# A message-passing layer on one core: attribute transfers issued at the landings of scatter pairs

## What is computed

```
row, col = src, dst
tp = fctp_messages(x[col], edge_attr, W1, W2, W3, W4)
messages = tp @ Wm + bm
agg = segment_sum(messages, row, num_segments=N_NODES)
upd = concatenate([x, agg], axis=-1) @ Wu + bu
out = layernorm(x + (x + upd))
```

## Time and profile before

| | us |
|---|---|
| median of 3 runs | 1928.22 (1927.52 to 1932.37) |
| profiled execution | 1923.78 |
| its span, first to last instruction | 1922.0 |
| PE busy | 1660.2 (86%) |
| DVE busy | 1549.8 (81%) |
| POOL busy | 1079.2 (56%) |
| ACT busy | 894.5 (47%) |

### The profile page before, as it was taken

One profiled execution on the slowest core, in us unless ns is written; L12 is line 12 of the kernel. 1 busy time (PEld: TensorE's weight loads), 2 busy tenths in 40 slices (PEclk: granted clock), 3 DMA queues, 4 the chain that ended last, 5 costly groups with the idle time before them and its releaser, 6 DMA issues.

```text
span 1922.0 us, 35044 instructions
## 1 busy us (share of the span) xinstructions
PE 1660.2 (86%) x11964; PEld 894.9 (47%) x11964; DVE 1549.8 (81%) x1727; ACT 894.5 (47%) x1721; POOL 1079.2 (56%) x837
## 2 busy tenths in 40 slices
PE   5439999999999999999999999999999999378883
PEld 2214444444444444444444444444444444266662
DVE  6347888888888888888888888888888886089994
ACT  1204444444444444444444444444444444168885
POOL 3106666766666666666666666666666665301110
PEclk9779999999999999999999999999999999789997
DMA  9996777777777777777777777777777774799994
GB/s 378 405 377 181 232 232 226 231 230 230 230 228 231 231 230 231 229 230 231 235 234 236 235 237 234 237 225 239 239 234 235 231 230 99 237 361 420 418 412 178
DMA packets 174616, 490.06 MB, mean 255 GB/s; under 512 B 48664, under 2 KB 99096, under 8 KB 149484
## 3 DMA queue, kind: packets, MB, share of 16 engines
q1 hardware_dynamic: 91980, 379.42, 51.6%
q0 software_dynamic: 82304, 109.12, 27.3%
q10 hardware_dynamic: 288, 0.95, 0.2%
HBM read 393.10 MB, written 96.31 MB: 255 GB/s over the span
## 4 chain that ended last, share of the span: by engine, by line
DMA 39%; issue 20%; POOL 20%; PE 11%; DVE 5%; ACT 2%; SPq 1%; POOLq 1%; ACTq 0%; DVEq 0%
DMA agg<-summed,row_idx 25%; POOL agg L324 14%; POOL xg L307 6%; DMA prod<-agg 5%; DMA xg<-in_x_rows,dst_sb 4%; DMA agg<-start_rows 4%; PE ps L648 3%; PE ps L641 2%; DVE stats L585 2%; DVE prod L566 2%; DMA e_sb<-in_e_rep 1%; ACT spread L365 1%; PE ps L694 1%; PE ps L629 1%; PE ps L695 1%
## 5 line engine op out<-in xcount | busy, mean ns | idle before, releaser
L324 POOL DMA_INDIRECT agg<-summed,row_idx x392 | 642.2, 1638 | 448.9 <-DMA agg<-summed,row_idx 294.0
L505 DVE TENSOR_TENSOR prod<-ps,e_sb 128x2048 f32<-128x2048 f32 x294 | 663.7, 2285 | 136.8 <-PE ps L648 132.2
L648 PE MATMUL ps<-prod,packed_sb 128*32 128x512 f32 x3136 | 752.7, 603 | 0.8 <-ACT S_sb L377 0.8
L307 POOL DMA_INDIRECT xg<-in_x_rows,dst_sb x392 | 410.5, 1047 | 179.4 <-issue 117.8
L641 PE MATMUL ps<-prod,packed_sb 128*32 128x512 f32 x2352 | 394.3, 600 | 0.0
L365 ACT ACTIVATE spread<-xg 128x1536 f32<-128x1536 f32 x98 | 145.5, 1485 | 424.1 <-DMA xg<-in_x_rows,dst_sb 413.5
L513 DVE TENSOR_TENSOR prod<-ps,e_sb 128x3072 f32<-128x3072 f32 x98 | 328.1, 3348 | 0.0
L493 DVE TENSOR_TENSOR prod<-ps,e_sb 128x2048 f32<-128x2048 f32 x98 | 223.9, 2285 | 108.6 <-ACT A_sb L371 69.4
L648 PEld LDWEIGHTS ps<-prod,packed_sb 128*32 128x32 f32 x3136 | 148.6, 109 | 156.7 <-issue 156.7
L629 PEld LDWEIGHTS ps<-packed_sb,spread 128*128 128x128 f32 x1176 | 127.3, 143 | 172.2 <-issue 123.6
L377 ACT ACTIVATE S_sb<-ps 128x512 f32<-128x512 f32 x98 | 58.7, 599 | 277.8 <-PE ps L648 277.8
(11 more groups left out here) (62 smaller groups left out, 1748.6 us busy)
## 6 DMA issues: line engine op xcount, KB each, us to landing
e_sb<-in_e_rep SPq DMA_DIRECT2D x98, 1536.0 KB, 7.2
e_sb<-in_e_rep SPq DMA_DIRECT2D x98, 1024.0 KB, 5.6
agg<-start_rows SPq DMA_DIRECT2D x49, 640.0 KB, 17.1
prod<-agg SPq DMA_DIRECT2D x48, 640.0 KB, 10.7
out<-prod POOLq DMA_DIRECT2D x48, 640.0 KB, 7.7
row_sb<-in_src_row SPq DMA_DIRECT2D x98, 256.0 KB
prod<-in_x_t SPq DMA_DIRECT2D x25, 640.0 KB, 11.8
e_sb<-in_x_t SPq DMA_DIRECT2D x24, 640.0 KB, 12.9
```

Source lines behind the costliest of these rows:

```text
L307: nc.gpsimd.indirect_dma_start(xg[g[1] % 2][:, q, :], None, x_rows, bass.IndirectOffsetOnAxis(dst_sb[g[1]][:, q:q + 1].bitcast(U32), 0)).t ...
L324: nc.gpsimd.indirect_dma_start(agg, bass.IndirectOffsetOnAxis(row_idx[g[1]][:, q:q + 1].bitcast(U32), 0), summed[g[1]][:, q // 2, q % 2 * ...
L505: nc.vector.tensor_tensor(prod[g[1] % 2][:, 4 + 4 * i:8 + 4 * i, :].rearrange("p (a b) e -> p a b e", b=2), ps[:, t_bank(g, 1 + i), :].uns ...
L648: return nc.tensor.matmul(ps[32 * quarter:32 * quarter + 32, S_BANK, :], w[:, 32 * half:32 * half + 32], prod[g[1] % 2][:, tile, :], start ...
```

## The change

SP's function `load_e` is split. `load_ev(g)` is issued one slot later than before, in slot g-1, ahead of `load_es(g+1)`. Both get a further wait, on scatters: es(g) waits from group 10 on until the second pair of group g-5 has landed, ev(g) from group 9 on until the first pair of group g-4 has landed. In slots: ev(s+1) waits for the first pair of s-3, es(s+2) for the second pair of s-3. The semaphore `scattered` becomes two, one for the first and one for the second scatter of each pair, and every wait on it becomes two waits. SP's loads wait on the second scatter's alone.

```
--- before.py
+++ after.py
@@ -159,7 +159,9 @@
         es_in = [sem(f"es_in{u}") for u in range(M1)]
         ev_in = [sem(f"ev_in{u}") for u in range(M1)]
         x_gathered = [sem(f"x_gathered{u}") for u in range(M1)]
-        scattered = sem("scattered")
+
+        scattered_a = sem("scattered_a")
+        scattered_b = sem("scattered_b")
         xT_in = [sem(f"xT_in{b}") for b in range(AHEAD)]
         agg_in = [sem(f"agg_in{b}") for b in range(AGG_BUFS)]
         nodes_out = [sem(f"nodes_out{b}") for b in range(Y_BUFS)]
@@ -210,14 +212,26 @@
 
         @block.sync
         def _(sp):
-            def load_e(g):
+            def load_es(g):
                 if at_least(g, 2):
 
                     sp.wait_ge(multiplied, number(g) * USES - 2 * USES + 4)
+                    hold(sp, sp_passed)
+                if at_least(g, 10):
+
+                    sp.wait_ge(scattered_b, number(g) * 32 - 5 * 32 + 32)
+                    hold(sp, sp_passed)
                 sp.dma_start(e_sb[g[1] % 2][:, 0:4, :], e_rep[number(g), :, 0:4, :].unsqueeze(0).to_broadcast([32, 4, 4, GE])
                              ).then_inc(es_in[g[1]], 16)
+
+            def load_ev(g):
                 if at_least(g, 2):
                     sp.wait_ge(multiplied, number(g) * USES - 2 * USES + 6)
+                    hold(sp, sp_passed)
+                if at_least(g, 9):
+
+                    sp.wait_ge(scattered_b, number(g) * 32 - 4 * 32 + 16)
+                    hold(sp, sp_passed)
                 sp.dma_start(e_sb[g[1] % 2][:, 4:ET, :], e_rep[number(g), :, 4:ET, :].unsqueeze(0).to_broadcast([32, 4, ET - 4, GE])
                              ).then_inc(ev_in[g[1]], 16)
 
@@ -247,8 +261,10 @@
                     load_dst(shift(s, 4))
                 if live(1):
                     load_src(shift(s, 1))
+                if live(1) and at_least(s, 1):
+                    load_ev(shift(s, 1))
                 if live(2):
-                    load_e(shift(s, 2))
+                    load_es(shift(s, 2))
                 if isinstance(s[0], int) and number(s) < 4:
                     for k in range(PIECES * (number(s) + 4) // 8, PIECES * (number(s) + 5) // 8):
                         start_table(k)
@@ -256,12 +272,14 @@
             sp.dma_start(start_rows[:, 0:D], bu.to_broadcast([P, D])).then_inc(start_rows_in, 16)
             for b in range(4):
                 load_dst((0, b))
-            load_e((0, 0))
+            load_es((0, 0))
+            load_ev((0, 0))
             load_src((0, 0))
             sp.wait_ge(start_rows_set, 1)
             for k in range(PIECES // 8):
                 start_table(k)
-            load_e((0, 1))
+            load_es((0, 1))
+            load_ev((0, 1))
             for k in range(PIECES // 8, PIECES // 2):
                 start_table(k)
             run_slots(sp, slot, 0, n_groups, 8, (n_groups - 4) // M1 * M1)
@@ -284,7 +302,8 @@
             for n in range(AHEAD):
                 load_xT(n)
 
-            sp.wait_ge(scattered, 16 * TILES * n_groups)
+            sp.wait_ge(scattered_a, 32 * n_groups)
+            sp.wait_ge(scattered_b, 32 * n_groups)
             def ahead(n):
 
                 return min(AHEAD + (n_out - AHEAD) * n // (n_out - 4), n_out)
@@ -316,14 +335,16 @@
                 if q % 2 == 0:
 
                     if at_least(g, 1) or q:
-                        pool.wait_ge(scattered, number(g) * 64 + q * 16)
+                        pool.wait_ge(scattered_a, number(g) * 32 + q * 8)
+                        pool.wait_ge(scattered_b, number(g) * 32 + q * 8)
                     else:
                         for u in range(PIECES_OUT):
                             pool.wait_ge(table_set[u], 16 * ((PIECES - u + PIECES_OUT - 1) // PIECES_OUT))
                     hold(pool, pool_passed)
                 nc.gpsimd.indirect_dma_start(
                     agg, bass.IndirectOffsetOnAxis(row_idx[g[1]][:, q:q + 1].bitcast(U32), 0),
-                    summed[g[1]][:, q // 2, q % 2 * MW:q % 2 * MW + D], None, compute_op=ALU.add).then_inc(scattered, 16)
+                    summed[g[1]][:, q // 2, q % 2 * MW:q % 2 * MW + D], None, compute_op=ALU.add
+                ).then_inc(scattered_b if q % 2 else scattered_a, 16)
 
             def slot(s):
                 live = lambda d: not isinstance(s[0], int) or 0 <= number(s) + d < n_groups
@@ -415,7 +436,8 @@
             def copy_summed(g):
                 act.wait_ge(summed_ready, number(g) + 1)
                 if at_least(g, 4):
-                    act.wait_ge(scattered, number(g) * 64 - 192)
+                    act.wait_ge(scattered_a, number(g) * 32 - 96)
+                    act.wait_ge(scattered_b, number(g) * 32 - 96)
                 nc.scalar.activation(summed[g[1]][:, :, :], msg_ps, ACT.Copy).then_inc(summed_copied, 1)
 
             def slot(s):
@@ -535,7 +557,8 @@
                 dve.wait_ge(idx_step, n * 2 + 1)
                 dve.wait_ge(src_in[g[1]], g[0] * 32 + 32)
                 if at_least(g, 4):
-                    dve.wait_ge(scattered, n * 64 - 192)
+                    dve.wait_ge(scattered_a, n * 32 - 96)
+                    dve.wait_ge(scattered_b, n * 32 - 96)
                 nc.vector.tensor_tensor(row_idx[g[1]][:, :], moved[:, :], src_sb[g[1]][:, :],
                                         ALU.max).then_inc(idx_step, 1)
```

## The result

The changed kernel is faster: a median of 1884.07 us (1881.23 to 1890.07, 4 runs) against 1930.3 (1927.52 to 1934.38, 4 runs), ratio 0.9763 with the interval 0.9732 to 0.9794. The prediction had 1838 and a range of 1815 to 1898. The time lies in the range, but the gain is half of the one forecast: the time is the one that the first rival gave, though not for its reason. The profiled execution took 1883.53, its span is 1881.7.

What follows compares the result with a forecast made beforehand. It took POOL's wait for scatter landings as the bound, TensorE's 14.82 us per group as the floor: span 1922.0 - 75.9 (loop) - 14.6 (tail) = 1831.5, plus 6.2 to the median, said as 1838; range 1815 to 1898.

Steps and rivals of the forecast that it cites:

- Rival 1: Edge loop: the serial chain of loads and scatters binds at 15.1 to 15.6 us per group; 1862 to 1906 us; chance 0.17.
- the floor: Edge loop: TensorE's matmuls set 14.82 us per group, against 15.84 before the change.
- (a): Edge loop: moving both loads cuts POOL's chain of two scatter pairs (A first, B second) from 15.7 to 13.9 us per group.
- (b): Edge loop, behind SP's new waits: late index transfers cost nothing; ev has 3.0 us slack if POOL runs in step.
- Rival 2: Edge loop: VectorE starves for ev, in a loop over two groups; slower, about 1983 us at 14 us per ev; chance 0.09.
- (c): First gated groups: getting into step costs once; group 10 starts at 243.6, group 97 at 1532.9, 75.9 us earlier.
- (d): Tail: scatters done at U+60 (U: group 97's first product start), gaining 14.6 us; node stage keeps its 238.6.
- (e): Start: ev of groups 2 to 5 comes some 13 us later; nothing taken, -4 to +6 us kept in the range.
- Rival 3: Edge loop: scatters and loads share the engines evenly, POOL's chain stays near 15.7; 1918 to 1934 us; chance 0.06.

Runs made afterwards that it cites:

- e4: Changed kernel, but from group 2 on es and ev each bring one tile of attributes instead of four and six; 1803.34 us.
- e6: Changed kernel with both load gates on the first scatter of a pair instead of the second; 1839.29 us, ratio 0.9532.
- e7: Changed kernel with its load gates on a semaphore that POOL itself increments after issuing a pair; 2093.52 us, ratio 1.087.
- e10: Changed kernel with a second 256 KB transfer of row_sb's bytes per slot, into an unread tile; 2005.68 us, ratio 1.04.
- e2: Changed kernel with the scatter gate on ev alone, none on es; 2029.78 us, ratio 1.0527.
- e3: Changed kernel with the scatter gate on es alone, none on ev; 2227.68 us, ratio 1.1553.
- e9: Changed kernel with src and row_sb transfers held until the first scatter of the slot's first pair has landed; 1971.55 us, ratio 1.0226.
- e12: Changed kernel with only ev's gate moved to the first scatter's landing, es's gate kept; 1845.87 us, ratio 0.9561.
- e8: Changed kernel, but from group 2 on VectorE's last product of a group computes two of its six tiles; 1882.21 us.
- e11: e6 with ev of groups 2 to 8 in its old place behind es; 1837.08 us, ratio 0.9523.

## Why the prediction was half right

- **What bounds the kernel before, and the floor:** right. 14.82 us is what PE needs (`e4`, `e6`: 14.81, 14.83).
- **(a) the chain of 13.9 us:** the step that failed. Its terms against the medians of the changed kernel: from A's start to the next pair's 6.43, measured 7.31, since A lands at 6.50 and not at 5.3; from B's start to the next pair's 7.45, measured 7.92, since B lands at 7.12 and not at 6.7. Together 15.2 instead of 13.9. The mechanism, a pair lands behind what was issued before it, was right and is shown by `e7`, `e10`, `e2` and `e3`; the list of what stands there was short, and the distance behind it too small. "es costs it nothing (18.75 + 0.5 = 19.25)" left out row_sb, which SP issues between es and the end of A's issue. With it A lands 0.45 behind row_sb. Without it, in `e9`, A lands at 5.75, so row_sb is 0.75 of A's excess; the rest is es itself, behind which A lands 1.0 there and not 0.5. B lands 0.88 behind ev, where 0.5 was taken: its first scatter lands 0.40 behind ev and its second 0.48 behind the first, since both stand behind the load, while in A only the second stands behind row_sb. That last reason is read from the landings and was not tested by a run. My section (b) had named the index transfers only as something that waits and can be late, not as bytes in the line.
- **A margin read as safe:** 0.9 us between two bounds, made of four readings, was less than the two errors together, 0.88 for A and 0.47 for B. Either alone would have left the chain just under the floor, at 14.8 or 14.4; `e12`, which takes away B's part, is at 14.89. Rival 1 named just this chain, and its 24 to 68 us over the forecast hold the measured 46; it had a chance of 0.17. That is luck in part: its reason, durations 0.7 us longer, was wrong: ev is 6.78 and es 5.32 in the median, shorter than the 7.2 and 5.6 taken.
- **(b) slack for ev of 3.0 us:** right as a limit, but used up. POOL's A starts 5.7 us after VectorE's group instead of 2.9, and VectorE waits for ev. Rival 2's loop is no bound (`e8`).
- **(c) getting into step:** group 10 at 243.6, measured 242.97. Group 97 at 1532.9, measured 1576.59: all 43.7 us are the term of (a).
- **(d) the tail:** U+60, measured 1643.5, U+67. Group 96's first scatter waited for the pair before it and came at 1611.59, U+35 instead of about U+27.5. But being late is not all: in `e6`, with POOL in step, it comes at U+29.3 and the scatters are still done only at U+66. The x_t loads go out from U+29.2 (here) and U+29.7 (`e6`), so they meet group 96's first pair too, which takes 10.4 us to the next start (11.0 in `e6`), where (d) had it clear. Here this was made good by group 97's first pair, clear in place of the 10 us taken for it. The node stage behind takes 238.2, forecast 238.6.
- **(e) the start:** +3.3 us for group 9, inside the -4 to +6; `e11` shows that it ends up as next to nothing.
- **Rival 3, sharing instead of a line:** its forecast fell. `e6` moves the same bytes as the changed kernel and takes 1839, far from 1918 to 1934. A load issued 1.1 us later cost 2.4 us per group (`e7`), and a pair behind two loads landed 9.6 to 10.8 us after its start, against 5.4 clear (`e2`, `e3`). The prediction set its rows against a rule of the Trainium skill, DMA: Bandwidth & Descriptors, Queues, rings and completion order, that each DMA engine goes round between the queues packet by packet. That was too strong. The packets show a line behind es in the changed kernel and the side by side that the rule describes in `e2`, and they do not tell how much of a load the rule counts as one packet; so the trace neither bears it out nor refutes it. What fell is the step from the rule to a time near the old one.

The forecast span, plus what the loop, the tail and the node stage took more or less: 1831.5 + 43.7 + 6.9 - 0.4 = 1881.7, the span measured. From the span to the median it was 2.4 us more and not the 6.2 taken, so the forecast is off by 46 us and not by 50.

## What to carry to other kernels

When a transfer is moved so that it no longer stands in front of another, write down everything that the same queue issues between the two, small index transfers included, before the new landing is summed up. A gate on one transfer is also a gate on all behind it in that queue: look at what it releases, and how close behind. And gate on the earliest event that comes after the protected transfer's issue: the first landing of a pair did in `e6` (1.3 us or more after the end of the pair's issue in the median of both pairs, never less than 0.3), the issuing engine's own increment did not. It is close: in a clear pair of `e2` the first landing is level with that end (3.47 and 3.50 us after the start).

## What the runs showed of the hardware

- A pair of indirect scatters lands, in the median of each kernel, 0.2 to 1.2 us after the last large transfer issued before the end of the pair's own issue, where that one is still under way: 0.45 (changed, A), 0.88 (changed, B), 0.50 (`e10`, one more in line), 0.24 (`e3`), 0.43 (`e2`), 1.24 (`e6`, A). Single pairs lie outside.
- While one load of 1024 KB is under way, no packet of a scatter issued behind it moves (changed kernel, 588.7 to 592.4 us); beside a second load they do (`e2`, 637.8 to 640.8).
- 256 KB of row_sb, one row of 2 KB repeated over 128 partitions, cost 1.25 us (ev's landing in `e9`) to 1.5 (`e10`), well over their share by bytes (0.8).
- A semaphore increment behind an indirect transfer on POOL was carried out at least 1.4 us before that transfer's own instruction began (`e7`).
